# First layer: keys, incidence sum and resets of the edge sorting on POOL, the wide copy of columns on ACT, instead of all on DVE

## The reference

```python
def _L0_gnn_ref(x, W, adj, bias):
    adj_0 = jnp.diag(jnp.diagonal(adj))
    adj_1 = jnp.triu(adj, k=1)
    adj_2 = jnp.tril(adj, k=-1)
    h = jnp.einsum('bjf,kfo->kbjo', x, W)
    out = jnp.einsum('ij,bjo->bio', adj_0, h[0]) + jnp.einsum('ij,bjo->bio', adj_1, h[1]) + jnp.einsum('ij,bjo->bio', adj_2, h[2])
    return out + bias[None, None, :]
h = jnp.maximum(_layernorm(x, axis=-1), 0.0)
x = x + _L0_gnn_ref(h, L0_gnn_W, adj, L0_gnn_bias)
```

```python
e = jnp.einsum('behd,hd->beh', jax.nn.leaky_relu(Qs + Kt, LRELU_SLOPE), a)
e = e + jnp.log(A0[src, dst] + EPS)[None, :, None]
m = jax.ops.segment_max(e_t, src, num_segments=n)
ex = jnp.exp(e_t - m[src])
denom = jax.ops.segment_sum(ex, src, num_segments=n)
Y = jax.ops.segment_sum(attn[..., None] * Vt, src, num_segments=n)
```

## Time and profile before

| | |
|---|---|
| median of 3 runs | 1201.83 us (1201.54 to 1202.85) |
| profiled execution | 1202.42 us, of it 1200.6 us span |
| PE busy | 1171.2 us, 98% |
| DVE busy | 982.8 us, 82% |
| ACT busy | 898.0 us, 75% |
| POOL busy | 433.0 us, 36% |
| first layer | from about 16 to 168 us of the span |
| sum of the first layer from 15 to 170 us (155 us): PE, DVE, ACT, POOL | 149.98, 123.73, 104.60, 111.83 us |

### The profile page before, as it was taken

One profiled execution on the slowest core, in us unless ns is written; L12 is line 12 of the kernel. 1 busy time (PEld: TensorE's weight loads), 2 busy tenths in 40 slices (PEclk: granted clock), 3 DMA queues, 4 the chain that ended last, 5 costly groups with the idle time before them and its releaser, 6 DMA issues.

```text
span 1200.6 us, 22233 instructions
## 1 busy us (share of the span) xinstructions
PE 1171.2 (98%) x7184; PEld 1015.1 (85%) x7184; DVE 982.8 (82%) x2049; ACT 898.0 (75%) x1725; POOL 433.0 (36%) x764
## 2 busy tenths in 40 slices
PE   8999999999899998999999999999999999999998
PEld 8999988864588886788878887898898899988997
DVE  7888859988788877888788878887887899998774
ACT  5766669978588878878687768877777688875554
POOL 4878747800177450000000000000000377778674
PEclk9999999999999999999999999999999999999999
DMA  8000000000311100000000000000300030001122
GB/s 328 2 1 2 2 1 1 0 1 0 114 71 70 61 36 1 1 1 1 1 1 1 1 1 1 1 1 1 141 1 1 2 140 1 1 2 53 71 78 81
DMA packets 14923, 38.21 MB, mean 32 GB/s; under 512 B 1904, under 2 KB 3952, under 8 KB 13808
## 3 DMA queue, kind: packets, MB, share of 16 engines
q1 hardware_dynamic: 14000, 36.60, 8.0%
q10 hardware_dynamic: 832, 0.46, 0.2%
HBM read 20.27 MB, written 16.78 MB: 31 GB/s over the span
## 4 chain that ended last, share of the span: by engine, by line
PE 63%; DVE 6%; ACT 2%; issue 1%; POOL 1%; POOLq 0%; DVEq 0%; ACTq 0%
PE psum L1306 7%; PE psum L1305 7%; PE psum L1307 7%; PE psum L1026 7%; PE psum L1334 5%; PE psum L1330 4%; PE psum L1331 4%; PE psum L1874 2%; PE psum L1623 2%; PE psum L1839 2%; PE psum L1049 2%; PE psum L1629 2%; PE psum L1849 2%; PE psum L1640 1%; PE psum L1860 1%; ACT gates L1351 1%
## 5 line engine op out<-in xcount | busy, mean ns | idle before, releaser
L1351 ACT ACTIVATE gates<-psum,lstm_bias 128x512 f32<-128x512 f32 (+1 forms) x504 | 301.9, 636 | 100.7 <-PE psum L1334 88.3
L193 POOL TENSOR_TENSOR l2r_sum<-l2r_st 128x8 f32<-128x8 f32 x16 | 5.1, 322 | 502.2 <-DVE l2r_st L129 501.9
L225 ACT ACTIVATE l_h<-X,nmr,rstd 128x128 f32<-128x128 f32 (+1 forms) x388 | 159.0, 484 | 11.7 <-DVEq L167 10.7
L1306 PE MATMUL psum<-lstm_node_hi,Wih_lo 128*128 128x512 f32 (+1 forms) x408 | 148.3, 364 | 0.0
L1307 PE MATMUL psum<-lstm_node_lo,Wih_hi 128*128 128x512 f32 (+1 forms) x408 | 147.9, 363 | 0.0
L1305 PE MATMUL psum<-lstm_node_hi,Wih_hi 128*128 128x512 f32 (+1 forms) x408 | 147.9, 363 | 0.0
L1330 PE MATMUL psum<-lstm_hid_hi,Whh_hi 128*128 128x512 f32 (+1 forms) x288 | 104.7, 364 | 3.9 <-DVE lstm_hid_hi L1413 3.7
L1334 PE MATMUL psum<-lstm_hid_lo,Whh_hi 128*128 128x512 f32 (+1 forms) x288 | 107.9, 375 | 0.0
L1331 PE MATMUL psum<-lstm_hid_hi,Whh_lo 128*128 128x512 f32 (+1 forms) x288 | 103.7, 360 | 0.0
L1361 ACT ACTIVATE gates<-lstm_cell 128x512 f32<-128x512 f32 (+1 forms) x144 | 83.7, 581 | 21.0 <-DVE lstm_cell L1400 20.6
L1305 PEld LDWEIGHTS psum<-lstm_node_hi,Wih_hi 128*128 128x128 f32 x408 | 77.2, 189 | 10.8 <-ACT gates L1351 0.3
(11 more groups left out here) (289 smaller groups left out, 3438.2 us busy)
## 6 DMA issues: line engine op xcount, KB each, us to landing
x_spill<-X SPq DMA_DIRECT2D x32, 256.0 KB, 2.0
X<-x_spill SPq DMA_DIRECT2D x2, 4096.0 KB, 13.2
out<-X SPq DMA_DIRECT2D x32, 256.0 KB, 2.0
X<-in_x SPq DMA_DIRECT2D x6, 1024.0 KB, 15.6
X<-in_x SPq DMA_DIRECT2D x3, 512.0 KB, 8.1
w_raw<-in_WihT SPq DMA_DIRECT2D x1, 1024.0 KB, 5.1
w_raw<-in_WhhT SPq DMA_DIRECT2D x1, 1024.0 KB, 7.4
X<-in_x SPq DMA_DIRECT2D x2, 256.0 KB, 3.3
```

Source lines behind the costliest of these rows:

```text
L225: last = act.activation(h[:, j, :], k.X[:, bass.ds(b0, TB), :][:, j, :], ACT.Relu, bias=k.nmr[:, bass.ds(b0, TB)][:, j:j + 1], scale=k.rst ...
L1306: pe.matmul(out, lo, x_high, start=False, stop=False)
L1351: act.activation(gate_of(it, g), k.bank[4 * s + g][:, 0:it.N], ACT.Tanh if g == GATE_G else ACT.Sigmoid, bias=k.lstm_bias[:, it.p - 1, g:g ...
```

## The change

The four instructions for the keys, `PT` and `reset` are no longer in DVE's `behind(i)` but in a function `edges(i)` on POOL, called at the end of POOL's iteration i, behind the coefficients for iteration i+2. DVE had one instruction for each key (multiply and add an array in one). POOL has two: a multiply with a constant, a wait, and an addition. The wide copy `colbc` goes to ACT, behind the normalisation for iteration 5. DVE waits for the keys (`keyed`) before RANK and PE for the wide copy (`widened`) before SORTED. All else keeps its place.

```diff
@@ block.gpsimd
+            def edges(i):
+                if i == KEYS:
+                    pool.wait_ge(as_float, 1)
+                    pool.wait_ge(iotas, 3)
+                    pool.tensor_scalar(key_row[:, :], row[:, 0, :], float(E), 0.0, ALU.mult, ALU.add)
+                    pool.tensor_scalar(key_col[:, :], col[:, 0, :], float(E), 0.0, ALU.mult, ALU.add).then_inc(keyed, 1)
+                    pool.wait_ge(keyed, 1)
+                    pool.tensor_tensor(out=key_row[:, :], in0=key_row[:, :], in1=order_row[:, :], op=ALU.add).then_inc(keyed, 1)
+                    pool.tensor_tensor(out=key_col[:, :], in0=key_col[:, :], in1=order_col[:, :], op=ALU.add).then_inc(keyed, 1)
+                if i == ROUND:
+                    pool.wait_ge(matched, 2)
+                    pool.tensor_tensor(out=e.PT[:, :], in0=ST[:, :].bitcast(F32), in1=DT[:, :], op=ALU.add)
+                if i == TURN:
+                    pool.wait_ge(cleared, 2)
+                    pool.tensor_scalar(e.reset[:, :], cont[:, :], -1.0, BIG, ALU.add, ALU.mult)
...
                 if i + AHEAD < n_it:
                     x_ln.coefficients(pool, i + AHEAD)
+                edges(i)
@@ block.scalar
+                if i == WIDE:
+                    act.wait_ge(as_float, 1)
+                    act.activation(colbc[:, :, :, :], col[:, :, :].unsqueeze(3).broadcast_to([P, 2, EC, P]), ACT.Copy).then_inc(widened, 1)
@@ block.tensor
                     pe.wait_ge(permed, EC)
+                    pe.wait_ge(widened, 1)
@@ block.vector
-                if i == KEYS:
-                    dve.wait_ge(as_float, 1)
-                    dve.wait_ge(iotas, 3)
-                    dve.scalar_tensor_tensor(key_row[:, :], row[:, 0, :], float(E), order_row[:, :], ALU.mult, ALU.add)
-                    chained(dve.scalar_tensor_tensor(key_col[:, :], col[:, 0, :], float(E), order_col[:, :], ALU.mult, ALU.add))
-                if i == WIDE:
-                    dve.tensor_copy(colbc[:, :, :, :], col[:, :, :].unsqueeze(3).broadcast_to([P, 2, EC, P]))
                 if i == RANK:
+                    dve.wait_ge(keyed, 3)
...
-                if i == ROUND:
-                    dve.tensor_tensor(e.PT[:, :], ST[:, :].bitcast(F32), DT[:, :], ALU.add)
...
-                if i == TURN:
-                    dve.wait_ge(cleared, 2)
-                    dve.tensor_scalar(e.reset[:, :], cont[:, :], -1.0, BIG, ALU.add, ALU.mult)
```

More of the change, by code:

```diff
@@ L286, in stage_first @@
     ST, DT, cont = sb("ST", [P, E], F32R), sb("DT", [P, E]), sb("cont", [P, E + 1])
-    A_ready = sem("l0_A")
+    A_ready, keyed, widened = sem("l0_A"), sem("edge_keyed"), sem("edge_wide")
     h_ready, hi_ready, lo_ready, T_ready, AB_ready, Z0_ready, Z12_ready, out_ready, biased, updated = (
```

## The result

The changed kernel took 1204.33 us, the median of 22 runs (1202.41 to 1206.10), against 1202.18 us for the kernel before in 22 runs on the same chip (1200.99 to 1203.13). The ratio is 1.0020, with a 95% interval of 1.0014 to 1.0027: slower, by 2.15 us in the medians. The profiled execution took 1204.09 us with a span of 1202.1, so 1.67 us and 1.5 us more than the one before (1202.42 and 1200.6).

What follows compares the result with a forecast made beforehand. PE, busy 98%, was taken as the bound, with POOL nearly full ahead of iteration 6. Lateness of 2.35 us there less 0.2 at `PT` gave +2.15 us on 1201.83: 1204.0 us, range 1201.5 to 1205.9.

Steps and rivals of the forecast that it cites:

- rival B: POOL's key multiply in iteration 3 costs 0.35 us instead of 1.07: +1.45 us in sum, 1203.3 us; chance 0.10.
- near 2: Sign at the first layer's end: the last update on DVE shifted by near 2 us, otherwise the prediction is wrong.
- The place and the mechanism: Iteration 6: keys on POOL make its coefficients late, with 0.56 us of slack; ACT waits, and the lag reaches PE.
- The lateness: Iteration 6: ACT and PE's second products 2.35 us late, from 2.3 us of key work plus collisions; bounds 1.1 to 3.7.
- My rule for them: DVE instructions with two SBUF inputs and POOL instructions reading SBUF exclude each other entirely; without it 0.5 us less.
- No credit for 0.72 us: The 0.72 us PE gains in iteration 4 doesn't reduce lateness in iteration 6; PE ahead only waits longer.
- The wide copy: Iteration 4: about 0.60 us on ACT, hidden before a wait with 1.4 us to spare; costs nothing.
- `PT`: Iteration 9: 0.73 us on POOL; PE gains 0.2 to 0.3 us in iteration 10, may be lost; taken as -0.2.
- `reset` and the new waits: Iteration 12: `reset` takes 1.07 us on POOL, delaying nothing; DVE's wait before RANK and PE's before SORTED cost nothing.
- A constant shift afterwards: After iteration 6 PE, DVE and ACT stay late by one amount; POOL takes up its lag in a 0.65 us wait.
- D: POOL stays the bound until iteration 14, one more 0.45 us collision per pair: +3.95 us, 1205.8 us; chance 0.13.
- C: PE's gaps in iterations 9 and 10 close, giving 0.7 us back: +1.45 us, 1203.3 us; chance 0.11.

Runs made afterwards that it cites:

- e1: The changed kernel with the keys back on DVE in iteration 3, the other moves kept; ratio 0.9997 to the kernel before.
- e3: The changed kernel with POOL's key instructions one iteration later, at the end of iteration 4; ratio 0.9994 to the kernel before.
- e6: The kernel before plus all four key instructions on POOL as idle work on unread tiles, DVE still doing its keys; ratio 1.0018 to the kernel before.
- e11: The changed kernel run again unaltered, for its groups of runs and a second profile; ratio 1.0021 to the kernel before.
- e4: The changed kernel with POOL's order swapped in even iterations, this layer's coefficients ahead of the next layer's; ratio 1.0015 to the kernel before.
- e2: The kernel before with only the four key instructions moved to POOL; ratio 1.0026 to the kernel before.
- e8: The kernel before with the wide copy on ACT, sorting stages one iteration later and RANK split over iterations 5 and 6; ratio 1.0011 to the kernel before.

## Why the prediction was right, and by what

The forecast was 1204.0 us with a range of 1201.5 to 1205.9; the median was 1204.33, and the shift that I summed, +2.15 us, is that of the medians. Part of this agreement is luck. All that I had summed lies in the first layer, and there the loss was 1.50 us, nearer to rival B's sum (+1.45) than to mine and short of the "near 2" that I had named as the sign. The other 0.65 us came from the groups of the runs, which I had not reckoned with.

**The place and the mechanism: right.** POOL's coefficients for iteration 6, 0.56 us from being what ACT waits for, became it. ACT starts 0.08 us after them (68.40 against 68.32), and the lag goes through `h_hi`, `h_lo`, RANK and `Z0` to PE unchanged: ACT is 1.83 us late (68.40 - 66.31 - 0.26), PE 1.85. e1 took the loss away, e3 took it from iteration 6 and left 0.4 us of it in iteration 8, e6 made 1.36 us of it with idle work alone.

**The lateness: 1.85 instead of 2.35.** Two terms were mis-sized. The multiply took 0.41 us and not 1.07; the four instructions with their wait made the bias of iteration 4 start 1.64 us late (55.38 - 53.48 - 0.26), where I had 2.3 for them and 0.5 for a collision. This is rival B's condition, and it came true. I was wrong to go by a row of the same shape with another operation, a maximum and an addition. (The Trainium skill, "GPSIMD Engine Reference", section 4.1, has one-input elementwise at roughly line rate, and was right on it.) Against that stood collisions. I had DVE's addition of `rows` held up by POOL's key addition; in fact it missed that one and met the bias, which took 0.54 us longer. From 57.20 to the end of the coefficients there are two more: an instruction at 58.87 took 0.73 us instead of 0.22, and one at 64.38 0.75 instead of 0.20. Their number and size were about as I had them, their places not. My rule for them was also too wide. I had one of the two engines stand still whenever DVE reads two inputs from SBUF, and a power on POOL does not do that to `h_lo` (rows in the last section).

**No credit for 0.72 us: right.** e6 decides it. With the gain the kernel came out even 0.5 us later than without it.

**The wide copy: right.** 0.62 us on ACT, with 1.52 us of idle time left behind it.

**`PT`: right.** 0.73 us on POOL, as priced. PE is 0.30 us less late in iteration 10 than in iteration 6 (1.55 against 1.85), at the upper end of the 0.2 to 0.3. ACT does not wait for the coefficients for iteration 12. **`reset` and the new waits:** nothing, as e1 shows with all of them in place but one. `reset` was priced by the same wrong row: it took 0.42 us on POOL and not 1.07.

**A constant shift afterwards: right for the layer**, with +1.55 in iteration 10 and +1.50 at the end, and D did not come. I had missed one gap of PE in the kernel before, 0.39 us in iteration 12 (0.27 in the changed kernel); it changed the sum by no more than 0.05. POOL took up its lag one place later than I said. At 69.73 it had no wait where I had expected 0.65 us to be used up; at 76.10 it waits 0.39 us again, and at 89.50 the full 0.64. C did not come either: the gap of iteration 9 is 0.52 us against 0.50.

**What I did not have: the clock.** More runs of the changed kernel lie in the upper groups: 1 of 22 and 0 of 7 (e11) in the lowest, against 11 of 22 of before. The profiles point to the fall of PE's clock near 482 us, and at a few other places in some executions, as what makes the groups. No run of the changed kernel's third group was profiled, so what makes that one is not shown. Why the upper groups are fuller in the changed kernel is open. The long wait in iteration 6 alone doesn't do it: e6 waits as long there (2.09 us) and has 3 of 10 runs in its lowest group (1202.20 to 1202.64), e4 waits 2.54 us and has 7 of 11 (1202.78 to 1203.07). Neither of them has the second wait, 0.73 us ahead of the first products, that the changed kernel, e11 and e2 have; whether that matters was not tested.

## What to carry to other kernels

Work moved to an engine with a low share lands at a place in its order: look at how long that engine has gone without a wait there, and how close its next product is to being the one waited for. Here 1.64 us on an engine of 36% made PE 1.85 us late, and the same instructions one iteration later made it late by 0.4 us, which the next gaps gave back. Count what stands behind the moved work, on every consumer, before choosing the place or swapping neighbours; and where two engines hold each other up, a shift moves the places where they meet: each such meeting was worth some 0.5 us here, either way. Before moving work, see if it can go into an instruction that is there anyway, as the factor went into ACT's conversion.

## What the runs showed of the hardware

- POOL's multiply of 128x256 with two constants took 0.41 us and `reset`, an addition and a multiply of 128x257, 0.42; a maximum and an addition of 128x256 took 1.07 us. So shape, type and number of constants don't fix the price. The row of 1.07 us also writes onto its own input and the other two don't; which of the two differences counts was not tested.
- Which of DVE and POOL stands still in a collision depends on who is first: DVE's two-input instructions took 0.97 to 1.56 us beside POOL's bias when it had begun, and POOL's bias 1.82 us when both began together at 55.38. The 128x512 ones of DVE ended 0.55 us after the bias (36.95 against 36.40 before, 158.63 against 158.08 in e8).
- Not every POOL instruction does this. In the kernel before, DVE's `h_lo` runs inside POOL's power seven times and takes 0.67 to 0.69 us each time, as without it. Iteration 4, timeline of POOL and DVE:

```profile
57.46 2.91 POOL L193 TENSOR_TENSOR l_m<-l_m,ln_const 128x16 f32<-128x16 f32 x1 [0.18 <-POOL l_m L193]
58.61 0.67 DVE L508 TENSOR_TENSOR l_h_lo<-l_h,l_h_hi 128x512 fp32r<-128x512 f32 x1
```

- Behind one wait of PE of 2.1 us the granted clock fell from the level of 2.4 GHz to that of 1.2 GHz for some 3 us in one profile (e2, 1.63 us lost), and behind waits as long in the changed kernel, e6 and e11 it didn't. (The Trainium skill, "TensorE: Matmul & The Clock Gate", Part 1, says of a kernel's start that how many matmuls run at the lower clock varies between runs of one kernel. Near 482, in the middle of the kernel, the two profiles of the changed kernel agree only weakly: the same 24 matmuls took 7.06 us in one and 7.27 in the other.)
